# A transformer megakernel on one Trainium2 core: the weights' split at a layer change in twelve pieces over six slots, the rotary tables rebuilt in two halves

## The chip, the cores and the metric

One core of a Trainium2 chip runs the whole program in one launch. The metric is the device time of one execution in microseconds (us), the median of several. The engines are PE (matrix products), DVE (vector), ACT (activation), POOL (GpSimd) and SP, which here only issues DMAs. Each works through its own instructions in program order. They wait for one another by counting semaphores.

## The reference, cut to what matters

The input is 8 sequences of 256 tokens with 128 channels. It is layer-normed; a causal attention with 16 heads of 64 and a stack of six layers both run on the normed input, and their results are added to the input.

```
xn = layernorm(x)
x  = x + causal_attention(xn) + stack(xn)

stack: for i in range(6):
    x = attn_layer(shift_tokens(x), Wqkv[i], q_scale[i], k_scale[i], Wo[i]) + x
    x = ffn_layer(shift_tokens(x), ln_g[i], ln_b[i], W1[i], b1[i], W2[i], b2[i]) + x

attn_layer: qkv = x @ Wqkv                    # [.., 128] @ [128, 3072]
    q = l2norm(q) * q_scale;  q = q*cos*scale + rotate_half(q)*sin*scale
    k = l2norm(k) * k_scale;  k = k*cos/scale + rotate_half(k)*sin/scale
    out = local_attention(q, k, v) @ Wo       # windows of 32, looking back one window
ffn_layer: (a * gelu(gate)) @ W2, from layernorm(x) @ W1
```

`shift_tokens` takes the upper half of the channels from the token before.

## The kernel before, in words

After a causal attention phase (to about 340 us) the six layers run as one software pipeline. Its unit of work is a **group**: one sequence and four heads, so 4 groups a sequence, 32 a layer, 192 in all. The pipeline advances in **slots**. Slot k starts group k+4 and carries on those begun before. The Python function `slot(k, r)` of each engine writes out what that engine does in slot k; slots 16 to 47 are the body of a loop that runs five times (TURNS, iteration r), so each loop body holds one layer change. By the slot's number in the layer, the new layer's first group is started in slot 28, its others of the first sequence in slots 29, 30 and 31.

In slot k:

- PE turns the weights of group k-1 (L759) and makes the scores of group k (L740, L749), multiplies the keys of group k+4 (L811, `project`), does two products of the output projection (L821), sums the norms of group k+3 (L826, which needs POOL's `sqs` of that group), weighs values (L773), does an MLP product in some slots, then the queries (L868) and the values (L870) of group k+4. The first matmul of the keys (L782, into `bank`) marks the start of a slot below.
- DVE shifts the scores (L997, L999), multiplies the keys with the rotary tables `tabs` (L1016, L1017: `rot_u`, `rot_v`), normalises the weights (L1004 to L1009), bounds the inverse norms (L1066: `rinv`, which lies in `probs_t`), and rotates the queries (again L1016, L1017).
- ACT raises the scores to exponentials (L552) and, behind that in its order, takes the logarithm and inverse root of the norms (L556, L559) and squares keys and queries.
- POOL adds the two parts of the rotated keys (`z_raw`, L406, two instructions), scales group k+3 by its norm (`z_norm`, L421, two), adds the squares (`sqs`, L427), and adds the rotated queries (`z_raw`, L406, two).
- SP moves `z_norm` into `zqk` by eight DMAs and the values into `v_late` by two.

The products of the projection are made from a high and a low part: `w_high` is the weight rounded to fp32r, `w_low` the rest. When a layer changes, POOL makes both anew, once for each of the four column groups g (`split_weights`, L397 and L399). The new weights have been fetched since slot 18 (L349). POOL splits group g at the end of its slot 25+g (L429 to L435), after the last use of the old columns (`lv_done`). PE waits for group g's split before the keys of slot 28+g (L809, L810). DVE builds the eight tables of 128x256 for the new layer at the end of its slot 27 (L1089, `rotary_tables`, L1025 to L1033): a small copy into `par_rot`, then for each of two query and two key tables two halves. Keys first need them in slot 28, queries at the end of the same slot.

For layer 0, POOL makes all four splits in a row before its slots begin (L440), and DVE its tables at L1100.

Of the kernel before, what the change touches and what calls it, by code (L numbers as in the profile page):

```python
# [7 lines left out]
F32 = mybir.dt.float32  # L8
BF16 = mybir.dt.bfloat16
F32R = mybir.dt.float32r  # L10
ALU = mybir.AluOpType
# [34 lines left out]
MLPS = UNITS // 2  # L46
FIRST, LOOP, LAST = -4, 16, GROUPS + 14
TURNS = DEPTH - 1


def block_of(slot, x):
# [53 lines left out]
def build(nc, x, w_kv_down, w_kv_up, w_q, w_out, Wqkv, q_scale, k_scale, Wo, ln_g, ln_b, W1, b1, W2, b2, const, out):  # L105
    with ExitStack() as ctx:  # L106
# [159 lines left out]
        def _(sp):  # L266
# [58 lines left out]
            def slot(k, r):  # L325
# [21 lines left out]
                if isinstance(r, int):  # L347
                    return
                if k == LAYER - 14:  # L349
                    sp.wait_ge(S["split_done"], G * (r + 1))  # L350
                    sp.sem_inc(S["room_met"], 1)
                    qkv_weights(r + 1)
                if LAYER - 1 <= k < LAYER - 1 + G:
# [29 lines left out]
        def _(pool):  # L383
# [7 lines left out]

            pool.memset(v_late[0:WIN, :, 0, :], 0.0).then_inc(S["spread_zero"], 1)

            def split_weights(l, g):

                cols = slice(g * GW, (g + 1) * GW)
                pool.tensor_copy(w_high[:, :, cols], w_qkv[:, :, cols]).then_inc(S["split_high"], 1)  # L397
                pool.wait_ge(S["split_high"], G * l + g + 1)
                pool.tensor_tensor(w_low[:, :, cols], w_qkv[:, :, cols], w_high[:, :, cols].bitcast(F32), ALU.subtract).then_inc(S["split_done"], 1)  # L399

            def rotated(m, parity, idx, prod, mark):

# [6 lines left out]
            def slot(k, r):  # L409
                s = LAYER * r + k  # L410
                one, two = active(k, r, -4, GROUPS - 4), active(k, r, -3, GROUPS - 3)
                if one:
                    rotated(s + 4, k % 2, 1, "k_prod", "k_summed")
                if two:

                    m, parity = s + 3, (k + 3) % 2
                    pool.wait_ge(S["bound_ready"], m + 1)
                    after(pool, f"z_in{(k + 1) % G}", 16 * 2 * HG * (unit_of(k + 1, r) + 1))
                    for idx, summed in ((1, "k_summed"), (0, "q_summed")):
                        pool.wait_ge(S[summed], m + 1)  # L420
                        a = pool.tensor_tensor(z_norm[:, parity, idx, :, :], rinv[:, idx, :].unsqueeze(1).broadcast_to([P, 2, T]), z_raw[:, parity, idx, :, :], ALU.mult)  # L421
                    a.then_inc(S["zn_ready"], 1)
                if one:
                    pool.wait_ge(S["k_square"], s + 5)
                    pool.wait_ge(S["q_square"], s + 5)
                    after(pool, "n_done", s + 4)
                    pool.tensor_tensor(sqs[:, :, :], sq[:, :, 0, :], sq[:, :, 1, :], ALU.add).then_inc(S["sums_ready"], 1)  # L427
                    rotated(s + 4, k % 2, 0, "q_prod", "q_summed")
                if not isinstance(r, int) and LAYER - 7 <= k < LAYER - 7 + G:  # L429
                    g = k + 7 - LAYER  # L430
                    if g == 0:
                        pool.wait_ge(S["w_in"], 16 * 3 * (r + 2))
                    pool.wait_ge(S["lv_done"], s + 4)
                    pool.sem_inc(S["split_begun"], 1)
                    split_weights(r + 1, g)  # L435

            pool.wait_ge(S["pv_done"], STEPS)
            pool.memset(spread[:, :, :, :], 0.0).then_inc(S["spread_zero"], 1)  # L438
            pool.wait_ge(S["w_in"], 16 * 3)
            for g in range(G):  # L440
                split_weights(0, g)
            stream(pool, slot)

        @block.scalar
# [163 lines left out]
        def _(pe):  # L608
# [188 lines left out]
            def slot(k, r):  # L797
# [7 lines left out]
                if one:  # L805
                    odd = (k + 4) // G % 2
                    if g == 0:
                        pe.wait_ge(S["x_split"], unit_of(k + 4, r) + 1)
                    if (k + 4) % LAYER < G:  # L809
                        pe.wait_ge(S["split_done"], G * ((k + 4) // LAYER + r) + g + 1)  # L810
                    project(s + 4, 1, B_K, g, odd, "lk_done", ("k_prod", "k_square"))  # L811
                if active(k, r, 2, GROUPS + 2):

# [95 lines left out]
        def _(dve):  # L909
# [112 lines left out]
                dve.wait_ge(S["x_high_ready"], unit + 1)  # L1022
                dve.tensor_tensor(x_low[:, odd, :], src, x_high[:, odd, :].bitcast(F32), ALU.subtract).then_inc(S["x_split"], 1)

            def rotary_tables(l):  # L1025
                dve.tensor_copy(par_rot[:, :], pars[:, 0:LG, ds(l, 1)].rearrange("p n a -> p (n a)")).then_inc(S["rot_par_ready"], 1)
                dve.wait_ge(S["rot_par_ready"], l + 1)
                for j, (c1, sign) in enumerate(((Q1, 1), (Q1, -1), (K1, 1), (K1, -1))):
                    for half in range(2):
                        m = dve.tensor_scalar(tabs[:, j, half, :], con("rot")[:, j * T:(j + 1) * T], par_rot[:, c1 + half:c1 + half + 1],  # L1030
                                              float(sign if half else 1), ALU.mult, ALU.mult)
                m.then_inc(S["tabs_ready"], 1)
                dve.wait_ge(S["tabs_ready"], l + 1)  # L1033

            def out_biases(l):
                dve.tensor_copy(out_bias[:, :], pars[:, B2:B2 + 4, ds(l, 1)].rearrange("p n a -> p (n a)")).then_inc(S["out_bias_ready"], 1)
# [2 lines left out]
            def slot(k, r):  # L1039
# [21 lines left out]
                    dve.tensor_tensor(xc[:, :], xc[:, :], rstd[:, :], ALU.mult).then_inc(S["xh_raw"], 1)  # L1061
                if three:
                    weigh_down(s)
                if two:
                    dve.wait_ge(S["rinv_ready"], s + 4)
                    dve.tensor_scalar(rinv[:, :, :], rinv[:, :, :], 1e12 / ROOT, None, ALU.min).then_inc(S["bound_ready"], 1)  # L1066
# [20 lines left out]
                if one:  # L1087
                    rotate(s + 4, 0, B_Q, "q_square", "q_summed", "q_prod")
                if not isinstance(r, int) and k == LAYER - 5:  # L1089
                    rotary_tables(r + 1)  # L1090
                if not isinstance(r, int) and k == LAYER + 15:
                    out_biases(r + 1)

# [3 lines left out]
            last_batch(causal, 0)  # L1097
            split_input(0, 0, 0)
            dve.wait_ge(S["pars_ready"], 1)
            rotary_tables(0)  # L1100
            out_biases(0)
            turn(causal, 0, ("post",))
            stream(dve, slot)
# [36 lines left out]
```

## Time and profile before

| | us |
|---|---|
| median of 3 runs | 2120.34 (2117.11 to 2122.38) |
| the profiled execution | 2116.4 |
| its span | 2114.6 |
| PE busy | 1982.1 (94%) |
| DVE busy | 1606.2 (76%) |
| ACT busy | 1398.1 (66%) |
| POOL busy | 1340.3 (63%) |

The profile is of one execution. A busy share is an average over the whole span; the layers' slots take 7.2 to 9.7 us each by the kind of work in them, with the same lengths in each layer, and a layer change takes place five times, near 601, 891, 1181, 1469 and 1758 us. The first of them is shown below. In a row of the timeline the bracket says how long the engine was idle before it and what ended that.

### The profile page before, as it was taken

How to read it: one execution, taken by the hardware profiler on the slowest of the kernel's cores; microseconds unless marked ns; L12 is line 12 of the kernel's file. 1: busy time of each engine (PE TensorE's matmuls, PEld its weight loads, DVE VectorE, ACT ScalarE, POOL GpSimd, SP SyncE). 2: the span in 40 equal slices, each digit the busy share in tenths (PEclk: the TensorE clock that was granted, in tenths of full speed). 3: DMA queues.
4: the chain of work that ended last, by engine and by line, in shares of the span. 5: the costliest groups of instructions: out<-in, count | busy, mean ns of one | idle time of the engine just before them, and what ended most of it. 6: DMA issues, size and time to landing. Idle time of an engine off the chain costs nothing. (4 is left out here: it accounts for less than half of the span.)

```text
span 2114.6 us, 70057 instructions
## 1 busy us (share of the span) xinstructions
PE 1982.1 (94%) x26905; PEld 1479.4 (70%) x26905; DVE 1606.2 (76%) x3109; ACT 1398.1 (66%) x2780; POOL 1340.3 (63%) x1402
## 2 busy tenths in 40 slices
PE   4999997999999989999989999999999899999995
PEld 3767665787767767777767677776777676777762
DVE  5666765787787867887867978688878688878773
ACT  2665653677757757676767577666777675777662
POOL 0000004987787767887767877678877678787750
PEclk9999998999999999999999999999999999999998
DMA  2000000444323334333343333343333433333330
GB/s 93 1 1 0 0 30 20 112 105 121 97 75 101 93 91 113 88 89 93 96 111 93 78 100 96 86 120 85 89 97 94 114 89 79 101 94 96 92 87 29
DMA packets 190633, 171.70 MB, mean 81 GB/s; under 512 B 32160, under 2 KB 186440, under 8 KB 190152
## 3 DMA queue, kind: packets, MB, share of 16 engines
q1 hardware_dynamic: 190280, 167.02, 30.1%
q8 instruction: 219, 3.59, 0.8%
q14 instruction: 134, 1.10, 0.2%
HBM read 21.14 MB, written 1.05 MB: 10 GB/s over the span
## 5 line engine op out<-in xcount | busy, mean ns | idle before, releaser
L406 POOL TENSOR_TENSOR z_raw<-rot_u,rot_v 128x256 f32<-128x256 f32 x768 | 551.0, 740 | 219.8 <-DVE rot_v L1017 217.4
L421 POOL TENSOR_TENSOR z_norm<-probs_t,z_raw 128x512 f32<-128x512 f32 x384 | 493.1, 1305 | 115.5 <-DVE probs_t L1066 115.5
L1016 DVE TENSOR_TENSOR rot_u<-bank,tabs 128x512 f32<-128x512 f32 x384 | 263.1, 685 | 202.2 <-ACT sq L520 198.8
L773 PEld LDWEIGHTS bank<-probs_t,v_late 128*64 128x64 f32 x3072 | 219.1, 136 | 146.6 <-issue 146.6
L782 PE MATMUL bank<-x_high,w_high 128*128 128x256 f32 x768 | 304.9, 397 | 3.4 <-issue 1.1
L552 ACT ACTIVATE pair_bank<-pair_bank 128x512 f32<-128x512 f32 x192 | 111.7, 582 | 259.4 <-DVE pair_bank L999 259.2
L520 ACT ACTIVATE sq<-bank 128x512 f32<-128x512 f32 x384 | 225.4, 588 | 76.8 <-PE bank L784 67.1
L773 PE MATMUL bank<-probs_t,v_late 128*64 128x64 f32 x3072 | 273.7, 234 | 0.5 <-ACT probs_t L539 0.5
L773 PE MATMUL bank<-probs_t,v_sb 128*64 128x64 f32 x3072 | 264.3, 222 | 0.0
L427 POOL TENSOR_TENSOR sqs<-sq 128x512 f32<-128x512 f32 x192 | 245.0, 1276 | 28.1 <-POOL z_norm L421 28.1
L1017 DVE TENSOR_TENSOR rot_v<-bank,tabs 128x512 f32<-128x512 f32 x384 | 261.4, 681 | 0.0
L539 ACT ACTIVATE probs_t<-bank 64x512 f32<-64x512 f32 x384 | 226.4, 590 | 40.4 <-PE bank L759 38.0
L826 PE MATMUL bank<-sqs,consts 128*128 128x512 f32 x384 | 207.2, 622 | 39.8 <-POOL sqs L427 37.1
L773 PEld LDWEIGHTS bank<-probs_t,v_sb 128*64 128x64 f32 x3072 | 219.8, 138 | 0.0
L783 PE MATMUL bank<-x_high,w_low 128*128 128x256 f32 x768 | 219.0, 285 | 0.0
L784 PE MATMUL bank<-x_low,w_high 128*128 128x256 f32 x768 | 218.6, 285 | 0.0
L438 POOL MEMSET probs_t<- 128x1024 f32 x1 | 1.0, 960 | 338.4 <-PE bank L677 338.4
L556 ACT ACTIVATE probs<-bank,tiny 128x512 f32<-128x512 f32 x192 | 131.9, 687 | 110.8 <-PE bank L826 109.8
L821 PE MATMUL bank<-yt,wo 128*128 128x256 f32 x768 | 203.0, 388 | 0.9 <-ACT yt L575 0.9
L782 PEld LDWEIGHTS bank<-x_high,w_high 128*128 128x128 f32 x768 | 147.5, 192 | 65.8 <-issue 47.7
L997 DVE TENSOR_REDUCE nm<-pair_bank 128x8 f32<-128x512 f32 x192 | 132.3, 689 | 71.4 <-PE pair_bank L749 70.1
L783 PEld LDWEIGHTS bank<-x_high,w_low 128*128 128x128 f32 x768 | 148.4, 193 | 38.4 <-issue 38.4
(153 smaller groups left out, 4541.3 us busy)
## 6 DMA issues: line engine op xcount, KB each, us to landing
zqk<-z_norm SPq DMA_DIRECT2D x1536, 64.0 KB, 2.1
v_late<-v_sb SPq DMA_DIRECT2D x192, 192.0 KB, 2.6
w_qkv<-in_L_ffn_Wqkv SPq DMA_DIRECT2D x18, 512.0 KB, 5.3
v_late<-v_sb SPq DMA_DIRECT2D x192, 32.0 KB, 2.2
wo<-in_L_ffn_Wo SPq DMA_DIRECT2D x24, 128.0 KB, 2.2
w<-in_L_ffn_W SPq DMA_DIRECT2D x12, 170.5 KB, 3.2
consts<-in_constants SPq DMA_DIRECT2D x1, 1088.0 KB, 5.2
w_qkv<-in_L_attn_w_kv_up SPq DMA_DIRECT2D x2, 512.0 KB, 6.3
```

Of the source, the lines that this page charges most:

```text
L406: a = pool.tensor_tensor(z_raw[:, parity, idx, half, :], rot_u[:, idx, half, :], rot_v[:, idx, 1 - half, :], ALU.add)
L421: a = pool.tensor_tensor(z_norm[:, parity, idx, :, :], rinv[:, idx, :].unsqueeze(1).broadcast_to([P, 2, T]), z_raw[:, parity, idx, :, :], ...
L427: pool.tensor_tensor(sqs[:, :, :], sq[:, :, 0, :], sq[:, :, 1, :], ALU.add).then_inc(S["sums_ready"], 1)
L520: act.activation(sq[:, idx, :, :], src[:, :].rearrange("p (a t) -> p a t", a=2), ACT.Square).then_inc(S[mark], 1)
L539: a = act.activation(spread[rows, :, :, WIN * x:WIN * x + WIN], tiles[rows, :, :, :], ACT.Copy)
L773: mm = pe.matmul(y[:, t, tile % 2, :, :], (v_sb if tile % 2 else v_late)[:, odd, t, f], spread[:, h, tile, :], start=True, stop=True, tile ...
L782: pe.matmul(dst, w_high[:, j, cols], x_high[:, odd, :], start=True, stop=False)
L783: pe.matmul(dst, w_low[:, j, cols], x_high[:, odd, :], start=False, stop=False)
L784: mm = pe.matmul(dst, w_high[:, j, cols], x_low[:, odd, :], start=False, stop=True)
L826: pe.matmul(B_N[:, :], con("blk"), sqs[:, :, :].rearrange("p a t -> p (a t)"), start=True, stop=True).then_inc(S["n_done"], 1)
L1016: dve.tensor_tensor(rot_u[:, idx, :, :], src, tabs[:, 2 * idx, :, :], ALU.mult)
L1017: dve.tensor_tensor(rot_v[:, idx, :, :], src, tabs[:, 2 * idx + 1, :, :], ALU.mult).then_inc(S[mark], 1)
```

## The change

**The split.** It is made in twelve pieces instead of four. A piece is one of keys, queries and values (in this order for each g, `PIECES`) for one column group: 128x256 instead of 128x768. POOL does two pieces at the end of each of the slots 25 to 30. Piece p belongs to group p // 3, so group 0 is complete after slot 26, group 1 after slot 27, group 2 with the first piece of slot 29 (piece 8) and group 3 with the second piece of slot 30 (piece 11). PE's wait before the keys of slot 28+g now asks for all three pieces of group g. SP's wait for room (L350) counts in pieces too. For layer 0 all twelve pieces stand in a row.

**The tables.** DVE makes the key tables (with the small copy) at the end of slot 27 as before, and the query tables in slot 28, after the weights are normalised and before the inverse norms are bounded.

```diff
-            def split_weights(l, g):
+            def split_weights(l, piece):
+                g, j = piece // 3, PIECES[piece % 3]
                 cols = slice(g * GW, (g + 1) * GW)
-                pool.tensor_copy(w_high[:, :, cols], w_qkv[:, :, cols]).then_inc(S["split_high"], 1)
-                pool.wait_ge(S["split_high"], G * l + g + 1)
-                pool.tensor_tensor(w_low[:, :, cols], w_qkv[:, :, cols], w_high[:, :, cols].bitcast(F32), ALU.subtract).then_inc(S["split_done"], 1)
+                pool.tensor_copy(w_high[:, j, cols], w_qkv[:, j, cols]).then_inc(S["split_high"], 1)
+                pool.wait_ge(S["split_high"], 3 * G * l + piece + 1)
+                pool.tensor_tensor(w_low[:, j, cols], w_qkv[:, j, cols], w_high[:, j, cols].bitcast(F32), ALU.subtract).then_inc(S["split_done"], 1)
...
-                if not isinstance(r, int) and LAYER - 7 <= k < LAYER - 7 + G:
-                    g = k + 7 - LAYER
-                    if g == 0:
+                if not isinstance(r, int) and LAYER - 7 <= k < LAYER - 1:
+                    at = 2 * (k + 7 - LAYER)
+                    if at == 0:
                         pool.wait_ge(S["w_in"], 16 * 3 * (r + 2))
-                    pool.wait_ge(S["lv_done"], s + 4)
+                    pool.wait_ge(S["lv_done"], LAYER * (r + 1) - 3 + (at + 1) // 3)
                     pool.sem_inc(S["split_begun"], 1)
-                    split_weights(r + 1, g)
+                    split_weights(r + 1, at)
+                    split_weights(r + 1, at + 1)
...
-            for g in range(G):
-                split_weights(0, g)
+            for piece in range(3 * G):
+                split_weights(0, piece)
...
                     if (k + 4) % LAYER < G:
-                        pe.wait_ge(S["split_done"], G * ((k + 4) // LAYER + r) + g + 1)
+                        pe.wait_ge(S["split_done"], 3 * (G * ((k + 4) // LAYER + r) + g + 1))
...
-            def rotary_tables(l):
-                dve.tensor_copy(par_rot[:, :], pars[:, 0:LG, ds(l, 1)].rearrange("p n a -> p (n a)")).then_inc(S["rot_par_ready"], 1)
-                dve.wait_ge(S["rot_par_ready"], l + 1)
-                for j, (c1, sign) in enumerate(((Q1, 1), (Q1, -1), (K1, 1), (K1, -1))):
+            def rotary_tables(l, which):
+                if which == 1:
+                    dve.tensor_copy(par_rot[:, :], pars[:, 0:LG, ds(l, 1)].rearrange("p n a -> p (n a)")).then_inc(S["rot_par_ready"], 1)
+                    dve.wait_ge(S["rot_par_ready"], l + 1)
+                c1 = (Q1, K1)[which]
+                for j, sign in ((2 * which, 1), (2 * which + 1, -1)):
...
+                if not isinstance(r, int) and k == LAYER - 4:
+                    rotary_tables(r + 1, 0)
                 if two:
...
                 if not isinstance(r, int) and k == LAYER - 5:
-                    rotary_tables(r + 1)
+                    rotary_tables(r + 1, 1)
```

POOL, before: the end of slot 28 with the last split (group 3), and slot 29 with none at its end.

```order
L406 TENSOR_TENSOR z_raw<-rot_u,rot_v 128x256 [waits zn_ready,q_prod]
L406 TENSOR_TENSOR z_raw<-rot_u,rot_v 128x256
L397 CAST w_high<-w_qkv 128x3x256 [waits lv_done]
L398 REGISTER_ALU
L399 TENSOR_TENSOR w_low<-w_qkv,w_high 128x3x256 [waits split_high]
L403 REGISTER_ALU
L406 TENSOR_TENSOR z_raw<-rot_u,rot_v 128x256 [waits zn_ready,k_prod]
L406 TENSOR_TENSOR z_raw<-rot_u,rot_v 128x256
L421 TENSOR_TENSOR z_norm<-probs_t,z_raw 128x512 [waits k_summed,z_in2,bound_ready]
L421 TENSOR_TENSOR z_norm<-probs_t,z_raw 128x512 [waits q_summed]
L427 TENSOR_TENSOR sqs<-sq 128x512 [waits n_done,q_square,k_square]
L406 TENSOR_TENSOR z_raw<-rot_u,rot_v 128x256 [waits zn_ready,q_prod]
```

POOL, now: slot 30 from its scaling of group 29 to its end, with pieces 10 and 11 (the lines of the code are two further down; slot 29 ends in the same way with pieces 8 and 9).

```order
L423 TENSOR_TENSOR z_norm<-probs_t,z_raw 128x512 [waits k_summed,z_in3,bound_ready]
L423 TENSOR_TENSOR z_norm<-probs_t,z_raw 128x512 [waits q_summed]
L429 TENSOR_TENSOR sqs<-sq 128x512 [waits n_done,q_square,k_square]
L408 TENSOR_TENSOR z_raw<-rot_u,rot_v 128x256 [waits zn_ready,q_prod]
L408 TENSOR_TENSOR z_raw<-rot_u,rot_v 128x256
L399 CAST w_high<-w_qkv 128x256 [waits lv_done]
L400 REGISTER_ALU
L401 TENSOR_TENSOR w_low<-w_qkv,w_high 128x256 [waits split_high]
L399 CAST w_high<-w_qkv 128x256
L400 REGISTER_ALU
L401 TENSOR_TENSOR w_low<-w_qkv,w_high 128x256 [waits split_high]
```

The last split stood at the end of POOL's slot 28; its last piece now stands at the end of slot 30, behind that slot's queries.

DVE, before: from the end of slot 27 to the bound of the norms in slot 28.

```order
L1030 TENSOR_SCALAR tabs<-consts,par_rot 128x256 x8
L997 TENSOR_REDUCE nm<-pair_bank 128x8
L999 TENSOR_TENSOR pair_bank<-pair_bank,nm 128x2x256
L1013 REGISTER_ALU
L1016 TENSOR_TENSOR rot_u<-bank,tabs 128x512
L1017 TENSOR_TENSOR rot_v<-bank,tabs 128x512
L1061 TENSOR_TENSOR xc<-xc,rstd 128x256
L1004 TENSOR_REDUCE rsum<-pair_bank 128x8
L1006 RECIPROCAL rrec<-rsum 128x8
L1009 TENSOR_TENSOR probs<-pair_bank,rrec 128x512
L1066 TENSOR_SCALAR probs_t<-probs_t 128x512
```

DVE, now: the same stretch.

```order
L1035 TENSOR_SCALAR tabs<-consts,par_rot 128x256 x4
L1038 ISA
L1000 TENSOR_REDUCE nm<-pair_bank 128x8
L1002 TENSOR_TENSOR pair_bank<-pair_bank,nm 128x2x256
L1016 REGISTER_ALU
L1019 TENSOR_TENSOR rot_u<-bank,tabs 128x512
L1020 TENSOR_TENSOR rot_v<-bank,tabs 128x512
...
L1012 TENSOR_TENSOR probs<-pair_bank,rrec 128x512
L1035 TENSOR_SCALAR tabs<-consts,par_rot 128x256 x4
L1038 REGISTER_ALU
L1073 TENSOR_SCALAR probs_t<-probs_t 128x512
```

Four of the eight table instructions have moved past the shift, the keys' rotation and the weights, to just before the bound.

## Rows read from the trace of the kernel before

**Rows 1.** Busy time by stretch: us, length, busy of each engine, PEclk, DMA share, GB/s

```profile
601.30:615.68 14.38, 11.39 (x133) 7.68 (x133) 14.21 (x21) 6.46 (x13) 10.20 (x10) 0.90 0.21 54
601.30:634.08 32.78, 29.79 (x390) 21.98 (x391) 28.42 (x46) 17.86 (x33) 27.47 (x28) 0.90 0.28 71
676.33:686.03 9.70, 9.70 (x133) 7.02 (x133) 7.74 (x14) 6.28 (x13) 6.90 (x8) 1.00 0.35 89
676.33:702.70 26.37, 26.37 (x390) 19.84 (x390) 21.60 (x38) 17.78 (x34) 20.02 (x22) 1.00 0.34 88
686.03:694.03 8.00, 8.00 (x133) 6.28 (x128) 7.63 (x14) 5.49 (x11) 4.88 (x6) 1.00 0.33 85
785.87:795.32 9.45, 9.45 (x128) 7.31 (x127) 5.57 (x11) 5.08 (x8) 3.94 (x4) 0.77 0.24 61
711.16:718.37 7.21, 7.21 (x127) 5.89 (x126) 6.35 (x11) 6.17 (x11) 5.20 (x7) 1.00 0.43 110
1468.71:1501.26 32.55, 29.55 (x390) 21.96 (x391) 28.53 (x46) 17.87 (x33) 27.46 (x28) 0.90 0.28 71
1758.07:1790.22 32.15, 28.59 (x390) 20.94 (x391) 28.65 (x46) 17.62 (x33) 27.46 (x28) 0.95 0.28 71
```

**Rows 2.** Timeline of PE at the layer change and at the loop's edge: start, us, operation

```profile
610.93 0.38 PE L792 MATMUL bank<-w_high,x_high 128*128 128x256 f32 x1 [1.37 <-ACT probs L556]
613.14 1.08 PE L759 MATMUL bank<-consts,probs 128*128 128x128 f32 x4 [1.24 <-ACT yt L575]
...
616.06 0.41 PE L783 MATMUL bank<-x_high,w_low 128*128 128x256 f32 x1
...
782.05 0.65 PE L759 MATMUL bank<-consts,probs 128*128 128x128 f32 x4 [3.83 <-issue]
```

**Rows 3.** Timeline of DVE, slots 27 and 28 of the first layer change

```profile
600.30 0.56 DVE L1026 COPY par_rot<-pars 128x4 f32 x1
600.89 7.31 DVE L1030 TENSOR_SCALAR tabs<-consts,par_rot 128x256 f32<-128x256 f32 x8
608.24 0.69 DVE L997 TENSOR_REDUCE nm<-pair_bank 128x8 f32<-128x512 f32 x1
...
612.66 0.42 DVE L1066 TENSOR_SCALAR probs_t<-probs_t 128x512 f32<-128x512 f32 x1
```

**Rows 4.** Timeline of ACT: the exponentials of slot 28

```profile
609.70 0.58 ACT L552 ACTIVATE pair_bank<-pair_bank 128x512 f32<-128x512 f32 x1 [7.30 <-DVE pair_bank L999]
```

**Rows 5.** Timeline of DVE cut at 604.5 us: the first four table instructions

```profile
600.89 4.07 DVE L1030 TENSOR_SCALAR tabs<-consts,par_rot 128x256 f32<-128x256 f32 x4
```

**Rows 6.** Instructions by line: ns min/median/max, first and last start us

```profile
L1030 DVE TENSOR_SCALAR tabs<-consts,par_rot x48: 341/812/1969, 336.9 to 1764.6; 128x256 f32<-128x256 f32 x48
L397 POOL CAST w_high<-w_qkv x24: 814/824/888, 342.4 to 1775.2; 128x768 fp32r<-128x768 f32 x24
L399 POOL TENSOR_TENSOR w_low<-w_qkv,w_high x24: 1802/1818/1836, 343.3 to 1776.1; 128x768 fp32r<-128x768 f32 x24
```

**Rows 7.** The page's costliest groups: POOL's addition of 128x256

```profile
L406 POOL TENSOR_TENSOR z_raw<-rot_u,rot_v 128x256 f32<-128x256 f32 x768 | 551.0, 740 | 219.8 <-DVE rot_v L1017 217.4
```

**Rows 8.** Timeline of POOL: slots 28, 29 and 30 of the change; a regular stretch

```profile
613.16 2.69 POOL L421 TENSOR_TENSOR z_norm<-probs_t,z_raw 128x512 f32<-128x512 f32 x2 [0.70 <-DVE probs_t L1066]
...
626.35 1.41 POOL L406 TENSOR_TENSOR z_raw<-rot_u,rot_v 128x256 f32<-128x256 f32 x2
...
633.94 1.41 POOL L406 TENSOR_TENSOR z_raw<-rot_u,rot_v 128x256 f32<-128x256 f32 x2
...
695.68 2.79 POOL L406 TENSOR_TENSOR z_raw<-rot_u,rot_v 128x256 f32<-128x256 f32 x4
```

**Rows 9.** Timeline of POOL at the start of the layers

```profile
342.41 0.83 POOL L397 CAST w_high<-w_qkv 128x768 fp32r<-128x768 f32 x1
...
353.08 1.64 POOL L406 TENSOR_TENSOR z_raw<-rot_u,rot_v 128x256 f32<-128x256 f32 x2
```

**Rows 10.** Timeline of PE there: the first sum of norms

```profile
356.09 1.41 PE L826 MATMUL bank<-sqs,consts 128*128 128x512 f32 x2 [2.86 <-POOL sqs L427]
```

More of the change, by code:

```diff
@@ L48 @@
 TURNS = DEPTH - 1
+PIECES = (1, 0, 2)
 def block_of(slot, x):
@@ L349, in slot @@
                 if k == LAYER - 14:
-                    sp.wait_ge(S["split_done"], G * (r + 1))
+                    sp.wait_ge(S["split_done"], 3 * G * (r + 1))
                     sp.sem_inc(S["room_met"], 1)
@@ L1032, in rotary_tables @@
                 m.then_inc(S["tabs_ready"], 1)
-                dve.wait_ge(S["tabs_ready"], l + 1)
+                dve.wait_ge(S["tabs_ready"], 2 * l + 2 - which)
             def out_biases(l):
@@ L1099, in _ @@
             dve.wait_ge(S["pars_ready"], 1)
-            rotary_tables(0)
+            rotary_tables(0, 1)
+            rotary_tables(0, 0)
             out_biases(0)
```

## The prediction

> **What bounds the kernel now.** I read the page's busy shares first, then cut PE's time into slots by the busy time of stretches, and then read the timelines of PE, DVE, ACT and POOL across the first layer change. Names of slots and pieces are those of the text above, "key start 29" is PE's first key matmul of slot 29.
>
> PE is busy 94% of the span, and in a regular stretch of three slots it never stops: 26.37 us busy of 26.37 [rows 1]. The three slots that hold a layer change (28 to 30) have the same work and take 32.78 us in the first change, 32.55 in the fourth and 32.15 in the last [rows 1] (the second and third lie near the last). So a change costs about 6.0 us there. The reader is to see where: slot 28 takes 14.38 us against 9.70 for the regular slot of its kind, while DVE is busy 14.21 of them. The cause is the eight table instructions, 7.31 us in one block, behind which the shift of the scores starts only at 608.24 [rows 3]. ACT stands idle 7.30 us for it [rows 4], and the logarithm and the output copy are queued behind that on ACT, for which PE waits 1.37 and 1.24 us [rows 2]. After that its matmuls take 0.41 us at a granted clock of 0.90 in the stretch; the clock is at its lower level for a while.
>
> The block is long by waiting, not by work. A table instruction takes 341 ns at best, 812 in the median and 1969 at worst [rows 6], and the first four take 4.07 us [rows 5] while POOL works. The Trainium skill (SBUF — State Buffer, "SBUF: two separate sides") says that such an instruction and one of POOL exclude each other from a shared port for a whole instruction; the long ones here, which end with POOL's, agree. By that rule alone the moved half costs little only where POOL stands idle.
>
> **The key half and what it frees.** The small copy and four instructions stay at the end of slot 27. POOL's splits at the ends of slots 25 and 26 shrink (below) by 0.43 us each, so I place the end of the half at 600.89 + 4.07 - 0.86 = 604.1 instead of 608.2. The shift starts 4.1 us earlier, and ACT and PE's two waits with it. PE then runs slot 28 in its regular 9.70 us: key start 29 comes near 610.5 instead of 615.68.
>
> **The query half.** From the shift's start to the bound of the norms lie 612.66 - 608.24 = 4.42 us [rows 3]; so the half begins at 604.1 + 4.42 = 608.5. POOL has then done its key addition and waits for the bound itself, so I take four times 341 ns, 1.36 us, and 0.42 for the bound: it ends at 610.30. The other end is the 4.07 us of the key half, 2.7 more. POOL's scaling waits for this.
>
> **The pieces.** POOL's addition of 128x256 takes 740 ns [rows 7], its subtraction of 128x768 1818 [rows 6]; the piece's subtraction has the form of the first, some 0.67 us from start to start. The cast of 768 columns takes 824 ns; a third is 0.27, and with a fixed part like the subtraction's (0.2 us by these two sizes) 0.41. With 0.08 for the wait between the two, a piece costs 1.02 to 1.16 us; I take 1.12, nearer the row of the same form. Two are 2.24 against 2.67 for a whole split (four take 353.08 - 342.41 = 10.67 [rows 9]), twelve 13.4.
>
> **What is late next.** This decides. PE's key start 30 now needs piece 8, at the end of POOL's slot 29, and key start 31 needs piece 11, at the end of POOL's slot 30. Behind that wait on PE stands everything of the slot: the key product, the output projection, the norms, the values. But PE starts the next slot's keys before POOL is done with the queries: in a regular stretch the key start at 694.03 [rows 1] lies before POOL's query addition ends, at 695.68 + 1.41 [rows 8], and key start 31 at 634.08 before 633.94 + 1.41 = 635.35. So both waits hold, each time.
>
> Key start 30: in the trace POOL needs 626.35 + 1.41 - 613.16 = 14.60 us from the scaling of slot 28 to the end of slot 29's queries [rows 8], with one whole split in it, nearly without idle time. With two pieces instead that is 14.16, piece 8 adds 1.12. From the bound's end at 610.30, and 0.08 to the scaling as in the trace: 610.38 + 14.16 + 1.12 = 625.66. Before it was 625.60. What the tables give is gone again, and PE, which could go on at 610.5 + 8.00 = 618.5 [rows 1], waits some 7 us in two places, for the norms and for piece 8.
>
> Key start 31: from key start 30 to the end of POOL's queries lie 635.35 - 625.60 = 9.75 us [rows 1, 8], and two pieces add 2.24: 637.65 against 634.08, 3.6 us later. The wait of some 5 us before will drop PE's clock; the norms and queries of slot 30 then come later, up to 1.4 us, and I take 0.7. In the other changes the old time is up to 0.6 shorter, with the same waits in the new: 0.4 in the mean. Together 4.7 us.
>
> After key start 31 PE has again stood for over 3 us. Such a stop of 3.83 us at the loop's edge [rows 2] is followed by a slot of 9.45 us at a granted clock of 0.77, of a kind that takes 7.21 [rows 1]: 2.24 us, of which I take half, since later slots have waits for POOL that swallow some. So 5.8 us for each of five changes, 29 us.
>
> **The start.** POOL's first addition stands behind all twelve pieces and PE waits for POOL (2.86 us [rows 10]); nothing hides the longer row: 13.4 - 10.67 = 2.7 us, between 1.6 and 3.2. The DVE tables of layer 0 are the same eight instructions.
>
> **The sum.** Profiled execution 2116.4 + 29 + 2.7 = 2148.1. The median of the runs is 3.9 above that execution, so I predict 2152. The added waits on DVE and SP are met when reached, and no DMA moves but those that follow POOL's scaling.
>
> **Rivals.**
>
> *The waits are short.* POOL catches up in slots 28 and 29. Its place is key start 30, its price this: key start 29 at 610.1, the 9.75 us to the end of the queries as in slot 30, a piece at 1.02, key start 30 at 620.9; then 9.75 + 2.04 to key start 31 at 632.7, 1.4 before the old 634.08, 1.0 in the mean of the changes, and no clock lost. Five times -1.0 and 1.6 for the start are -3.4: 2117, no slower. It decides from where POOL has more than 3 us of idle time between its scaling of slot 28 and its queries of slot 29. Against it: POOL is busy nearly all the 14.60 us there. Chance 0.06.
>
> *The gain alone.* The waits for the pieces never hold and each change is regular: 5 x 6.0 us less, 2.7 more, 2093. It needs POOL's queries to end before PE's next key start, which no place above shows. Chance 0.04.
>
> *The query half is blocked as the key half is.* If POOL is still in pieces or its key addition when the half starts, it costs up to 2.7 us more; POOL's chain, both key starts and PE's clock follow: 5 x 2.7 more, 2165. For it: every table instruction of a block that meets a working POOL is long [rows 5, 6]. Against: POOL has nothing to do without the bound once the key addition is through. Chance 0.17.
>
> *POOL is the one that is blocked.* By the same page the lock works the other way too: DVE's table instructions in a row could hold POOL. The cast of a split, which falls into the tables' block, takes 888 ns at most against 824 in the median [rows 6]; with a few hundredths for each, this moves nothing, and I give it no chance of its own.
>
> **Chances and range.** The forecast has 0.73, with its own range from 2141 to 2160: the piece's price moves it by 0.6 us a change, the clock by 1. For all cases 2132 to 2170: the low end takes in a catch-up by half, the high end the blocked half with the full price of the clock. No change means within 0.3%, 6.4 us, about what a measurement of this kernel can tell. Faster 0.04, same 0.06, slower 0.90.
>
> **What would show it.** In the new trace, per change: the key tables in about 4 us and the query tables in about 1.4; slot 28 near 9.7 us; PE idle before key starts 30 and 31 with POOL's w_low as what ended it, some 5 and 3.5 us; POOL almost without idle time from slot 28 to key start 30; a lower clock after each wait; POOL's twelve pieces at the start in about 13.4 us. Wrong: slots 28 to 30 together under 32 us, or no wait of PE for POOL's pieces. I would be wrong altogether if POOL's queries of slot 29 ended before PE is ready for the keys of slot 30.

## The result

The changed kernel takes 2164.2 us in the median of 6 runs (2161.39 to 2168.16), against 2120.17 for the kernel before in the same runs: a ratio of 1.0215, with a 95% interval from 1.0198 to 1.0232. It is 44 us slower. The forecast was 2152, slower, with a range to 2170; 2164 lies inside that range, but above the forecast's own range of 2141 to 2160.

The page of the changed kernel shows PE with the same 26905 matmuls, and idle in a place where it had none before. The columns of the group are those of the page's costliest groups; the last figure is the idle time before the group and what ended most of it.

```profile
PE 1995.4 (92%) x26905; PEld 1490.5 (69%) x26905; DVE 1587.6 (73%) x3109; ACT 1400.1 (65%) x2780; POOL 1354.5 (63%) x1498
...
L785 PE MATMUL bank<-x_high,w_high 128*128 128x256 f32 x768 | 306.7, 399 | 44.0 <-POOL w_low L401 41.7
```

L785 is the first matmul of a projection's product, of keys or queries. The same group on the page of the kernel before:

```profile
L782 PE MATMUL bank<-x_high,w_high 128*128 128x256 f32 x768 | 304.9, 397 | 3.4 <-issue 1.1
```

Before the change PE had stood idle for 3.4 us there in the whole run; now 44.0, of which 41.7 end with a piece of the split.

Across the first layer change, PE's busy time by stretch, from key start to key start (slots 28, 29, 30 and 31, and the three first together; the columns are as in [rows 1]):

```profile
604.29:614.55 10.26, 10.20 (x133) 6.99 (x133) 10.02 (x20) 6.03 (x13) 7.30 (x11) 1.00 0.29 75
614.55:629.94 15.39, 8.29 (x129) 6.20 (x129) 12.05 (x19) 6.35 (x12) 14.79 (x19) 0.92 0.27 69
629.94:644.25 14.31, 10.54 (x131) 7.98 (x131) 6.22 (x11) 5.89 (x10) 9.49 (x13) 0.85 0.25 62
644.25:654.31 10.06, 10.06 (x130) 7.69 (x131) 4.50 (x8) 5.30 (x10) 5.09 (x5) 0.83 0.19 50
604.29:644.25 39.96, 29.03 (x391) 21.17 (x391) 28.29 (x49) 18.27 (x34) 31.58 (x41) 0.91 0.27 68
```

Slot 28 has fallen from 14.38 us to 10.26; slots 29 and 30 have risen, and the three together went from 32.78 [rows 1] to 39.96. In slot 29 POOL is busy 14.79 of 15.39 us, and PE 8.29.

PE's timeline there, the rows with idle time and the first after them:

```profile
618.21 1.10 PE L829 MATMUL bank<-sqs,consts 128*128 128x512 f32 x2 [1.84 <-POOL sqs L429]
...
629.94 0.55 PE L785 MATMUL bank<-x_high,w_high 128*128 128x256 f32 x1 [5.26 <-POOL w_low L401]
630.29 0.41 PE L786 MATMUL bank<-x_high,w_low 128*128 128x256 f32 x1
...
644.25 0.36 PE L785 MATMUL bank<-x_high,w_high 128*128 128x256 f32 x1 [3.77 <-POOL w_low L401]
```

The two waits of the old kernel (for ACT, 1.37 and 1.24 us [rows 2]) are gone; three others have come, 10.9 us together. Behind the long ones a matmul takes 0.41 us again.

DVE, the two halves of the tables (the copy and the shift after the first half, the bound after the second), which answer to [rows 3]:

```profile
603.47 1.31 DVE L1030 COPY par_rot<-pars 128x4 f32 x1
604.82 3.18 DVE L1035 TENSOR_SCALAR tabs<-consts,par_rot 128x256 f32<-128x256 f32 x4
608.03 0.69 DVE L1000 TENSOR_REDUCE nm<-pair_bank 128x8 f32<-128x512 f32 x1
...
612.46 1.14 DVE L1035 TENSOR_SCALAR tabs<-consts,par_rot 128x256 f32<-128x256 f32 x4
613.63 0.43 DVE L1073 TENSOR_SCALAR probs_t<-probs_t 128x512 f32<-128x512 f32 x1
```

Four such instructions take 3.18 us beside a working POOL and 1.14 beside one that waits.

POOL, from the scaling in slot 28 over piece 8 to piece 11, which answers to [rows 8]:

```profile
614.14 2.70 POOL L423 TENSOR_TENSOR z_norm<-probs_t,z_raw 128x512 f32<-128x512 f32 x2 [1.88 <-DVE probs_t L1073]
...
627.16 1.40 POOL L408 TENSOR_TENSOR z_raw<-rot_u,rot_v 128x256 f32<-128x256 f32 x2
628.50 0.40 POOL L399 CAST w_high<-w_qkv 128x256 fp32r<-128x256 f32 x1
628.98 0.72 POOL L401 TENSOR_TENSOR w_low<-w_qkv,w_high 128x256 fp32r<-128x256 f32 x1
...
632.97 1.41 POOL L408 TENSOR_TENSOR z_raw<-rot_u,rot_v 128x256 f32<-128x256 f32 x2 [2.12 <-DVE rot_v L1020]
636.60 2.52 POOL L423 TENSOR_TENSOR z_norm<-probs_t,z_raw 128x512 f32<-128x512 f32 x2 [2.22 <-DVE probs_t L1073]
...
643.28 0.72 POOL L401 TENSOR_TENSOR w_low<-w_qkv,w_high 128x256 fp32r<-128x256 f32 x1
```

Piece 8 ends at 628.98 + 0.72 = 629.70, and key start 30 follows at 629.94; piece 11 at 644.00, and key start 31 at 644.25.

At the start of the layers the twelve pieces run from 342.33 to 356.33, 14.0 us against 10.67 [rows 9], and POOL's first addition behind them:

```profile
342.33 0.40 POOL L399 CAST w_high<-w_qkv 128x256 fp32r<-128x256 f32 x1
...
356.33 1.40 POOL L408 TENSOR_TENSOR z_raw<-rot_u,rot_v 128x256 f32<-128x256 f32 x2
```

The table below gives the lengths of the slots at a layer change as means over the five, each from key start to key start in PE's timeline of the profiled execution, for all kernels whose runs are told below. In e13 the key starts 30 and 31 are those of the key products, behind the extra matmuls. The regular slots of these kinds (those that follow eight groups later) sum to 34.8 for slots 28 to 31, and slot 27's to 8.5.

```
kernel                              median  slot 27   28     29     30     31   28 to 31
before                              2120.2    9.5   14.3    9.0    9.0    8.4    40.8
changed                             2164.2    9.2   10.3   15.4   13.9    9.9    49.5
e1 tables in halves alone           2107.1    9.5   10.4    9.9    9.8    8.4    38.5
e2 split in pieces alone            2171.3    9.2   12.7   14.1   14.3   10.0    51.0
e3 changed, PE waits by the piece   2111.6    9.2   10.3   10.4    9.4    8.7    38.8
e4 changed, first split whole       2155.4    9.2   10.3   15.4   14.1    9.3    49.0
e5 changed, pieces a slot earlier   2110.9    9.0   10.3   11.3    8.7    8.6    38.9
e6 before, two whole splits late    2173.9    9.5   11.3   15.2   14.3   10.7    51.5
e7 changed, pieces 8, 9 in slot 28  2154.9    9.1   10.3   10.4   15.8   10.9    47.4
e9 e1, whole splits a slot earlier  2108.2    9.5   10.4    9.9    9.1    8.4    37.8
e10 e9, query half after the bound  2124.8    9.5   10.4   12.5    9.1    8.5    40.4
e11 e9, tables where POOL waits     2106.7   11.4    9.8    8.2    9.0    8.4    35.4
e13 changed, PE kept busy           2149.2    9.2   10.2   15.4   12.1    8.5    46.2
```

The changed kernel loses 8.4 us at each change (slots 27 to 31: 58.6 against 50.3), 42 in all, and 3 at the start.

Each ratio below is to the kernel before as run beside that experiment: its median was 2118.4 us beside e1 to e4, 2115.5 beside e5, e6, e7 and e9, and 2116.0 beside e10, e11 and e13. A difference of a few us between medians of different sets is therefore not a finding; there the slots in the table decide.

### The profile page after: what moved, and what is told of

Its sections match the earlier page's. It is cut to its first block and busy times, and to the rows that moved or that the text cites. A ratio compares the mean times of both kernels' runs of the same rounds, so it can differ in the third digit from the quotient of the medians.

```text
span 2160.7 us, 70233 instructions
## 1 busy us (share of the span) xinstructions
PE 1995.4 (92%) x26905; PEld 1490.5 (69%) x26905; DVE 1587.6 (73%) x3109; ACT 1400.1 (65%) x2780; POOL 1354.5 (63%) x1498
## 5 line engine op out<-in xcount | busy, mean ns | idle before, releaser
L785 PE MATMUL bank<-x_high,w_high 128*128 128x256 f32 x768 | 306.7, 399 | 44.0 <-POOL w_low L401 41.7
L785 PEld LDWEIGHTS bank<-x_high,w_high 128*128 128x128 f32 x768 | 149.4, 195 | 106.9 <-issue 89.4
L824 PE MATMUL bank<-yt,wo 128*128 128x256 f32 x768 | 209.7, 398 | 0.9 <-ACT yt L578 0.9
```

The costliest lines, as they stand in the source:

```text
L785: pe.matmul(dst, w_high[:, j, cols], x_high[:, odd, :], start=True, stop=False)
L824: mm = pe.matmul(B_X[:, 0:T], wo[:, c, :], yt[:, c, :], start=(c == 0), stop=(c == HD // P - 1))
```

## The experiments

**e1, the tables in halves alone.** The split stays as before.

```diff
 (against the kernel before; rotary_tables takes `which` as in the change)
...
-                    rotary_tables(r + 1)
+                    rotary_tables(r + 1, 1)
...
                 if three:
                     weigh_down(s)
+                if not isinstance(r, int) and k == LAYER - 4:
+                    rotary_tables(r + 1, 0)
...
```

> The tables in two halves, the split whole as before. Theory (PE's two waits for pieces 8 and 11, and the clock after them, are the loss): no wait for the split before key starts 30 and 31; slots 28 to 30 take 28 to 30 us instead of 32.4, so 2095 to 2110 us, clearly faster than before. Rival (the query half of the tables, now ahead of the norms' bound, is the loss): no faster than before, 2120 us or more, with POOL late in slot 29.

Measured: 2107.1 us, ratio 0.9958 (0.9940 to 0.9976). This half of the change is a gain, small but clear of the noise, and the rival is out. Slots 28 to 31 fell from 40.8 to 38.5 us; I had expected slots 28 to 30 at 28 to 30, and they take 30.1. Slot 28 gave 4.0 us, but slots 29 and 30 took 1.7 back, in waits for the norms:

```profile
604.78 1.10 PE L826 MATMUL bank<-sqs,consts 128*128 128x512 f32 x2 [0.37 <-POOL sqs L427]
616.44 1.10 PE L826 MATMUL bank<-sqs,consts 128*128 128x512 f32 x2 [1.66 <-POOL sqs L427]
625.76 1.10 PE L826 MATMUL bank<-sqs,consts 128*128 128x512 f32 x2 [1.03 <-POOL sqs L427]
```

**e2, the split in pieces alone.** The changed kernel with `rotary_tables` and its calls as before.

> The split in twelve pieces over six slots, the tables whole as before. Theory: both waits stay, and POOL's chain to piece 8 starts about 1 us later than in the changed kernel, since the eight table instructions stand ahead of the scores' shift: 2162 to 2175 us. Rival (the query half is the loss): at most 2130 us.

Measured: 2171.3 us, ratio 1.0261 (1.0226 to 1.0296). All of the loss and more comes from the split; slot 28 lacks the tables' gain, and PE waits 5.26 and 3.76 us at the two key starts as in the changed kernel.

**e3, PE waits by the piece.** POOL's order is untouched.

```diff
 (against the changed kernel, PE)
-                    if (k + 4) % LAYER < G:
-                        pe.wait_ge(S["split_done"], 3 * (G * ((k + 4) // LAYER + r) + g + 1))
+                    fresh = (k + 4) % LAYER < G
+                    split_before = 3 * (G * ((k + 4) // LAYER + r) + g)
+                    if fresh:
+                        pe.wait_ge(S["split_done"], split_before + 1)
                     project(s + 4, 1, B_K, g, odd, "lk_done", ("k_prod", "k_square"))
...
                 if one:
+                    if fresh:
+                        pe.wait_ge(S["split_done"], split_before + 2)
                     project(s + 4, 0, B_Q, g, odd, "lq_done", ("q_prod", "q_square"))
                 if one:
+                    if fresh:
+                        pe.wait_ge(S["split_done"], split_before + 3)
                     values(s + 4, g, odd)
```

> The changed kernel, but PE waits for each piece where it is used: before the keys for the group's key piece, before the queries for the query piece, before the values for the value piece. POOL's work and order are unchanged. Theory (it is the wait at the key start, not the pieces): key start 30 needs piece 6 and key start 31 piece 9, both long done; no PE stop at either; slots 28 to 30 take 27 to 29 us, total 2095 to 2112 us. Rival (more and longer POOL work in six slots is the loss): stays above 2150 us.

Measured: 2111.6 us, ratio to the kernel before 0.9971 (0.9949 to 0.9994), 53 us below the changed kernel. The pieces, their number and their slots are the same; only what PE asks for at a key start differs. Slots 28 to 30 take 30.1 us, where I had expected 27 to 29: PE's waits for the norms stay. In PE's timeline from 610 to 645 us two waits are left, both for the norms:

```profile
618.32 1.10 PE L831 MATMUL bank<-sqs,consts 128*128 128x512 f32 x2 [1.81 <-POOL sqs L429]
627.49 1.10 PE L831 MATMUL bank<-sqs,consts 128*128 128x512 f32 x2 [0.86 <-POOL sqs L429]
```

Against e1, which has the same tables and the four whole splits (2107.1 us, 38.5 us in slots 28 to 31), e3 is not faster (2111.6, 38.8). The pieces have lost their cost here; no gain of theirs is to be seen.

**e4, layer 0's split whole.** The changed kernel with four pairs of instructions of 768 columns ahead of the slots.

> The changed kernel with layer 0's split whole (four of 768 columns instead of twelve of 256). Theory: POOL's first addition starts 3.3 us earlier and all that follows with it, about 3 us in all, near 2160 us; each layer change as in the changed kernel. Rival (PE's wait there is absorbed later): no difference.

Measured: 2155.4 us, once. One time cannot tell 3 us; the trace can. From the first key start to the ninth lie 56.5 us, as in the kernel before (56.5), against 59.6 in the changed one, a difference of 3.1 us; the layer changes are near those of the changed kernel (49.0 us for slots 28 to 31). But the first key start itself moves by up to 3 us between executions. From the first split instruction to the ninth key start lie 62.5 to 65.5 us in the seven kernels that split layer 0 whole, and 66.8 to 67.9 in the six with pieces; the means differ by 3.4. So the start costs about 3 us, and a tenth can't be told.

**e5, the pieces a slot earlier.**

```diff
-                if not isinstance(r, int) and LAYER - 7 <= k < LAYER - 1:
-                    at = 2 * (k + 7 - LAYER)
+                if not isinstance(r, int) and LAYER - 8 <= k < LAYER - 2:
+                    at = 2 * (k + 8 - LAYER)
```

> The changed kernel with its pieces in slots 24 to 29 instead of 25 to 30, PE's waits as in the changed kernel. Theory (the place of pieces 8 and 11 behind PE's key start is the loss): both are done a slot before PE asks, so no stop before key starts 30 and 31, slots 28 to 31 near the 38.8 us of the kernel with finer waits, 2103 to 2117 us. Rival (PE's asking for three pieces at once is the loss wherever they stand): over 2150 us.

Measured: 2110.9 us, ratio 0.9977 (0.9964 to 0.9990). PE asks for three pieces at once as in the changed kernel, and waits for none at a layer change: moving them by one slot does as much as asking for less.

**e6, whole splits late.** The kernel before, with groups 2 and 3 split at the ends of slots 29 and 30.

```diff
 (against the kernel before)
-                if not isinstance(r, int) and LAYER - 7 <= k < LAYER - 7 + G:
-                    g = k + 7 - LAYER
+                if not isinstance(r, int) and k - LAYER in (-7, -6, -3, -2):
+                    g = (-7, -6, -3, -2).index(k - LAYER)
...
-                    pool.wait_ge(S["lv_done"], s + 4)
+                    pool.wait_ge(S["lv_done"], LAYER * (r + 1) - 3 + g)
```

> The kernel before (tables whole, splits whole) with the splits of groups 2 and 3 moved to the ends of slots 29 and 30. Theory (place, not number): each stands behind the queries of its slot and PE waits for it at key starts 30 and 31 as in the changed kernel; 2155 to 2175 us. Rival (the number and form of the pieces is the loss): within 10 us of the kernel before.

Measured: 2173.9 us, ratio 1.0285 (1.0257 to 1.0313). The same two waits appear without any piece:

```profile
628.79 0.55 PE L782 MATMUL bank<-x_high,w_high 128*128 128x256 f32 x1 [6.22 <-POOL w_low L399]
643.07 0.55 PE L782 MATMUL bank<-x_high,w_high 128*128 128x256 f32 x1 [4.12 <-POOL w_low L399]
```

With e3 and e5 this settles it: the place behind which PE must wait makes the loss, not the number of the pieces.

**e7, one wait instead of two.** Pieces 8 and 9 move up to the end of slot 28.

```diff
-                    pool.wait_ge(S["lv_done"], LAYER * (r + 1) - 3 + (at + 1) // 3)
+                    pool.wait_ge(S["lv_done"], LAYER * (r + 1) - 3 + (at + 1 + 2 * (at == 6)) // 3)
                     pool.sem_inc(S["split_begun"], 1)
-                    split_weights(r + 1, at)
-                    split_weights(r + 1, at + 1)
+                    if at != 8:
+                        split_weights(r + 1, at)
+                        split_weights(r + 1, at + 1)
+                    if at == 6:
+                        split_weights(r + 1, 8)
+                        split_weights(r + 1, 9)
```

> The changed kernel with pieces 8 and 9 moved up to the end of slot 28, behind 6 and 7; 10 and 11 stay at the end of slot 30. Theory: key start 30 no longer waits for a piece, key start 31 still does. If the lower clock after the first wait is what stretches the way from key start 30 to the end of POOL's queries from 9.8 to 11.8 us, slot 30 is now near 12 to 13 us and the kernel 4 to 5 us per change faster than the changed one: 2136 to 2148 us. Rival (one wait costs as much as two, since POOL's chain sets the end anyway): above 2155 us.

Measured: 2154.9 us, ratio 1.0177 (1.0149 to 1.0205). The time lies between what the theory and the rival had named, and next to the rival's. The medians put it 9 us below the changed kernel, but the kernel before was 5 us faster in this set too; by the slots it is 2.1 us a change (47.4 against 49.5), where I had 4 to 5. Slot 29 gave back 5.0 us, slot 30 took 1.9 more and slot 31 1.0. The reason stands in two rows: without the first wait PE is ahead, and POOL, with four pieces in slot 28, is behind by more when its slot 30 begins; PE then waits for the norms and for piece 11.

```profile
629.43 1.10 PE L833 MATMUL bank<-sqs,consts 128*128 128x512 f32 x2 [2.93 <-POOL sqs L429]
640.10 0.55 PE L789 MATMUL bank<-x_high,w_high 128*128 128x256 f32 x1 [3.76 <-POOL w_low L401]
```

So POOL's chain to piece 11 is what counts, as the rival had it: with one wait left, some 43 of the 53 us that e3 saves are still lost. It says nothing clean about the clock; e13 was made for that.

**e13, PE kept busy in the waits.** The extra matmuls stand ahead of PE's wait at key starts 30 and 31 and write the bank that the key product overwrites.

```diff
                     if (k + 4) % LAYER < G:
+                        if not isinstance(r, int) and g in (2, 3):
+                            for name in ("k_prod", "k_square"):
+                                after(pe, name, s + 4)
+                            for _ in range({2: 34, 3: 24}[g]):
+                                pe.matmul(B_K[:, 0:T], w_high[:, 1, 0:P], x_high[:, odd, :], start=True, stop=True)
                         pe.wait_ge(S["split_done"], ...)
```

> The changed kernel with 34 extra matmuls of 256 columns before PE's wait at key start 30 and 24 before that at key start 31 (results overwritten), so that PE works through most of both waits. Theory (the clock's lower level after each stop is what my sum took too small): the granted clock stays at its upper level, the way from key start 30 to the end of POOL's queries is 9.8 to 10.2 us instead of 11.3, slot 31 near 8.5 us instead of 9.9; 12 to 17 us faster than the changed kernel, 2146 to 2154 us. Rival (the way is longer because the norms' product stands behind PE's wait): 2158 us or more.

Measured: 2149.2 us, ratio 1.0149 (1.0124 to 1.0175), 15 us below the changed kernel (14 by the ratios), inside what was expected. Slots 29, 30 and 31 of the first change:

```profile
615.22:630.52 15.30, 12.55 (x163) 10.30 (x163) 12.04 (x19) 6.34 (x12) 14.69 (x19) 1.00 0.27 69
630.52:642.65 12.13, 11.58 (x154) 9.55 (x155) 6.22 (x11) 5.90 (x10) 9.72 (x13) 1.00 0.27 69
642.65:651.16 8.51, 8.47 (x130) 6.56 (x131) 4.50 (x8) 5.34 (x10) 5.15 (x5) 1.00 0.25 67
```

The granted clock is 1.00 in all three. Slot 29 is as long as in the changed kernel, since PE still waits for piece 8; slot 30 is 2.2 us shorter and slot 31 1.6. From key start 30 to the end of POOL's queries lie 9.78 us, against 11.78 in the changed kernel and 9.75 in the kernel before. In the means over the five changes it is 13.9 - 12.1 and 9.9 - 8.5, together 3.2 us a change: this is what the lower level of the clock costs here. What is left of the two waits (0.92 and 0.55 us) still ends with a piece, as in the changed kernel.

**e9, whole splits a slot earlier.** e1 with the four whole splits at the ends of slots 24 to 27.

```diff
 (against e1)
-                if not isinstance(r, int) and LAYER - 7 <= k < LAYER - 7 + G:
-                    g = k + 7 - LAYER
+                if not isinstance(r, int) and LAYER - 8 <= k < LAYER - 8 + G:
+                    g = k + 8 - LAYER
...
-                    pool.wait_ge(S["lv_done"], s + 4)
+                    pool.wait_ge(S["lv_done"], LAYER * (r + 1) - 3 + g)
```

> The tables in halves, the splits whole, but one slot earlier (slots 24 to 27), so that slot 28 of POOL has none. Theory (in the tables-alone kernel the split at the end of POOL's slot 28 is on the chain to the norms of slots 29 and 30): slots 28 to 31 take 36 to 38 us instead of 38.5, 2095 to 2105 us. Rival (it is hidden there): as the tables-alone kernel, 2107 us.

Measured: 2108.2 us, ratio 0.9962 (0.9950 to 0.9974). The trace shows the gain in slot 30 (9.1 against 9.8), 0.7 us a change. Slots 28 to 31 take 37.8 us, as expected, but the time misses the 2095 to 2105 of the theory and lies at the rival's: the medians can't tell it from e1.

**e10, the query half after the bound.** e9 with the four query tables one instruction later.

> Tables in halves, splits whole in slots 24 to 27, the query half behind the norms' bound instead of ahead of it. Theory (1.1 us of the query half stand on the chain to the norms of slot 29): slot 29 about 1 us shorter, but the four instructions now run beside POOL's scaling and take 2.5 to 3 us; in sum 0 to 5 us faster than with the half ahead of the bound, 2103 to 2108 us. Rival (their waiting delays the input's split and the queries' rotation, and POOL with them): 2110 to 2118 us.

Measured: 2124.8 us, ratio 1.0037 (1.0024 to 1.0050), 17 us slower than e9 (16 by the ratios); a miss in sign. Beside POOL's scaling and its addition of the squares the four take 4.20 us instead of 1.13:

```profile
609.30 0.42 DVE L1068 TENSOR_SCALAR probs_t<-probs_t 128x512 f32<-128x512 f32 x1
609.63 4.20 DVE L1032 TENSOR_SCALAR tabs<-consts,par_rot 128x256 f32<-128x256 f32 x4
614.02 0.29 DVE L1021 CAST x_high<-xs 128x256 fp32r<-128x256 f32 x1 [0.20 <-DVE tabs L1032]
```

Everything behind them on DVE in slots 28 and 29 is late, and slot 29 has grown to 12.5 us. The rival had this mechanism, but its range ended at 2118 us.

**e11, all tables where POOL waits.** e9 with the copy, the key tables and the query tables each ahead of the bound, in slots 26, 27 and 28.

```diff
 (against e9; the small copy is now `rotary_scales`)
                 if three:
                     weigh_down(s)
+                if not isinstance(r, int) and k == LAYER - 6:
+                    rotary_scales(r + 1)
+                if not isinstance(r, int) and k == LAYER - 5:
+                    rotary_tables(r + 1, 1)
                 if not isinstance(r, int) and k == LAYER - 4:
                     rotary_tables(r + 1, 0)
...
-                if not isinstance(r, int) and k == LAYER - 5:
-                    rotary_tables(r + 1, 1)
```

> The splits whole in slots 24 to 27, and the tables only where POOL waits for the norms' bound: the small copy in slot 26, the key tables in slot 27, the query tables in slot 28, each behind the weights of its slot. Theory (table instructions are long only beside a working POOL, so the key half costs 1.1 us instead of 4.5, and slot 28 gets back to near 9.7 us): slots 28 to 31 take 36 to 37 us, 2096 to 2105 us. Rival (the key half now delays the bound of slot 27 and the norms of slot 28 by the same amount): as the kernel with whole splits a slot earlier, 2108 us.

Measured: 2106.7 us, ratio 0.9953 (0.9934 to 0.9973). Slots 28 to 31 are down to 35.4 us, 0.6 from the regular 34.8, but slot 27 is up from 9.5 to 11.4, so that it is no faster than e1 or e9 as far as can be measured. The place is not one where POOL waits: in slot 27 it is still at the split of slot 26 and the key addition, so the four key tables take 3.20 us (the query tables in slot 28 2.08, beside the key addition), and hold back DVE's part of the MLP (`hid`), for which PE then waits 2.05 us. The rival's sum was right, by another way than the one it named.

```profile
596.84 3.20 DVE L1033 TENSOR_SCALAR tabs<-consts,par_rot 128x256 f32<-128x256 f32 x4
```

```profile
601.30 0.67 PE L887 MATMUL bank<-xc,consts 128*128 128x256 f32 x2 [2.05 <-DVE hid L1094]
```

## Why the prediction was right, and where its sum was short

**The mechanism held.** PE waits for piece 8 at key start 30 and for piece 11 at key start 31, at every change; e2 and e6 make the waits without the tables and without the pieces, e3 and e5 take them away. The tables' gain in slot 28 is there (10.3 us, forecast 9.7) and is gone by key start 30, as forecast. The rivals are out: POOL didn't catch up, the waits hold, and the query half took 1.14 us, not 4. PE's waits ahead of key start 30 are 1.84 and 5.26 us in the first change, where the sum had some 7 in two places.

**The sum was 32 us, the measured loss 44.** The time lies within 1 us of 2165, the price that the prediction gave the blocked query half; that is chance, since this half was not blocked. By the steps of the sum:

- *The start*: forecast 2.7, measured about 3 (e4; POOL's row itself is 3.3 longer). A piece takes 1.15 us, forecast 1.12, and one cast was stretched to 0.60 us beside DVE.
- *Key start 30 from key start 28*: forecast 625.66 - 600.8 = 24.9 us (600.8 is key start 29 at 610.5 less a slot of 9.70), measured 629.94 - 604.29 = 25.65. The key half ended later against key start 28 (3.7 us behind it, forecast 3.3), because its copy began only 0.8 us ahead of that key start, where my sum had 1.4: I had moved the half up by the 0.86 us that POOL saves. Its length is nearly the old one, copy and four instructions 4.53 us against 4.66 [rows 3, 5]: the copy now meets POOL's second scaling (1.31 us instead of 0.56), and the four meet one such instruction less (3.18 instead of 4.07). POOL's way from the scaling to the end of slot 29's queries took 14.42 us, forecast 14.16. And a wait ends 0.24 us after the piece does, which I had left out, twice a change.
- *Key start 31 from key start 30*: forecast 12.0 with a fast clock and 12.7 with my allowance; measured 14.31 in the first change and 13.85 in the mean. This is the mis-sized term. With PE kept busy it is 12.13 (e13), so the part without the clock was right to 0.13 us and the clock's was 1.7 in the mean, not 0.7.
- *Behind key start 31*: forecast 1.1, measured 1.5 in slot 31 (9.93 against 8.43), and 1.4 of it goes when PE is kept busy.

I had the row for the clock's price, 2.24 us after one stop [rows 1], and took half of it for the second stop and 0.7 for the first. In e13 the two give back 3.2 us a change, against the 1.8 that I had taken: 7 of the missing 12 us over five changes. Another 4 are what the way to key start 30 was short by, 0.8 us a change, and 1 is slot 27, which became 0.3 us shorter where I had 0.5.

## What to carry to other kernels

Work that is moved to a later place is late for the engine that asks for it first, even if the slot's number says that it is in time: compare the end of the moved work with the start of its user's wait in the trace, not slot with slot. If work is cut into pieces and moved late, let the user wait by the piece: here that alone was worth 53 us. That made the pieces harmless, not useful; the kernels with pieces and no wait for them (e3 2111.6, e5 2110.9 us) are no faster than those with whole splits and the same tables (e1 2107.1, e9 2108.2). Of the two edits of a change, look at each alone: the tables in halves gain 0.4% (2107 us), the pieces in their slots lose 2.6%.

## What the runs showed of the hardware

- A DVE instruction of this kind with both sides in SBUF takes 0.28 us in a row by itself (1.13 to 1.14 for four). Beside a working POOL each costs one of POOL's instructions: in e10 the four took 0.35, 1.37, 1.37 and 1.35 us, the first begun with POOL still idle, the others beside two scalings (1.32 and 1.33) and the addition of the squares (1.31), and each ended 0.14 to 0.16 us after POOL's. What the four cost hangs on which of POOL's instructions they meet, not on their own size.
- A copy of 4 columns, which took 0.16 us with POOL idle (layer 0, kernel before), took 0.56 us beside it before the change and 1.31 in the changed kernel, where it met a scaling.
- POOL pays little for it: its two scalings took 2.61 us in e10 beside the tables, and 2.52 in the same execution's next slots without them.
- Two stops of PE of 5.3 and 3.8 us cost 3.2 us more in the work behind them, at the lower of the clock's two levels (1.2 GHz); matmuls whose results nobody reads bought this back.
